# A decoder with 64 routed experts on one core: the final weighted sum divided among PE, VectorE and GpSimd, and the experts' transfers sent by SyncE in the order of the tiles

## The chip, the cores and the metric

The kernel runs on one core of a Trainium2 chip. The metric is the time on the device, in microseconds, of the whole program: two decoder layers, the second of which ends in a mixture of experts. The engines are named as in the profile: PE is the tensor engine, DVE is VectorE, ACT is ScalarE, POOL is GpSimd, SP is SyncE, which here only sends transfers. ACT and POOL can send transfers too; a "q" behind a name (SPq, ACTq) marks an engine's own queue of instructions. The kernel before took 856.12 us in the median of three runs.

## The reference, cut to what matters

Six blocks follow each other, each with a residual and a normalisation: attention, cross attention, a feed-forward block (layer 0), attention, cross attention, and the experts (layer 1). The change touches the last one alone. There are 1024 tokens (8 sequences of 128), 256 columns, 64 experts, and each token goes to its 8 best.

```python
logits = jnp.einsum('th,eh->te', x, gate_w)
probs = jax.nn.softmax(logits, axis=-1)
topk_w, topk_idx = jax.lax.top_k(probs, 8)
combine = (jax.nn.one_hot(topk_idx, 64) * topk_w[..., None]).sum(axis=1)
for each expert e:
    g = x @ w13_e[:128].T
    u = x @ w13_e[128:].T
    o = (silu(g) * u) @ w2_e.T
    acc = acc + combine[:, e][:, None] * o
x = layernorm(x + acc)
```

## The kernel before

Every token's row is scattered by POOL to `x5_slots` in device memory, into the 1024 places that each expert has there. The experts then work on tiles of 128 places. There are 127 tiles: one for each of the 64 experts (its first 128 places) and 63 extra ones, whose expert and first place a plan computes on PE and DVE while the first tiles run. An extra tile that the plan has no use for is given an address beyond the end; its transfers are conditional and are then skipped. PE does each tile's work all the same.

`ORDER` is the order of the tiles. The weights of 32 experts (`KEPT`) lie in SBUF from earlier stages. The other tiles, 32 own tiles of experts and 63 extra ones, get their weights (384 KB) through eight slots (`SLOTS`, tiles `w_slot`); `LOADS` lists them in order. Tiles 5 to 19 alternate between kept experts and the first eight loaded ones. Tiles 20 to 67 mix kept experts with 28 extra tiles. From tile 68 on, 24 own tiles with loaded weights are mixed with 35 extra ones, so every tile there loads weights. The input rows (136 KB) lie in six buffers (`WORK`).

PE's step j (`pe_experts`, L1702 on) transposes tile j (`turn`), multiplies tile j-1 by its first weights (`up`) and tile j-3 by its second (`down`). ACT copies the transposed rows and computes silu, DVE takes the product, picks the tokens' places (`pick`) and copies the result, and POOL scatters 128 rows to `y_slots`, one row for each of the 8 choices of each token.

Who sends what before the change:
- SP (`sp_experts`, L1680 on) sends the first eight weight blocks and the rows of tiles 0 to 5. Then it waits for the plan's table (`lines_set`) and goes over the extra tiles: it reads an address (`value_load`, L1695), sends that tile's weights once the eighth load before it has left its slot, and the rows of an extra tile j after the weight block whose slot belonged to tile j-8 (`AHEAD`).
- ACT (`act_experts`, L1744 on) sends the rows of the 58 own tiles from tile 6 on, five tiles ahead of its own place, and the weights of the 24 own tiles, five tiles after their slot's last user.

`load_rows` (L1664 on) waits until the buffer's last rows were transposed and picked; `load_weights` (L1657 on) until the slot's last `down` is done.

At the end, `sp_combine` waits for all scatters and sends eight transfers of 1 MB, one for each sequence: for every token its 8 rows from `y_slots`. The weighted sum is made on PE (`pe_combine`): ACT makes for each row index j a diagonal matrix of 128 weights, and PE adds the eight products of diagonal and rows in PSUM. DVE (`dve_combine`) adds the residual, takes statistics and their aggregate and adds epsilon (`begin`, lines L1899, L180, L182, L184). POOL takes the root (L188). DVE scales (`end`, L192), after the `begin` of the next sequence, and ACT sends the result out. Four lanes (`SUMS`) of buffers and PSUM banks are used in turn.

## Time and profile before

| | |
|---|---|
| median of 3 runs | 856.12 us (854.72 to 858.25) |
| the profiled execution | 856.72 us |
| its span on the core | 855.3 us |
| busy: PE, DVE, ACT, POOL | 769.4 us (90%), 531.2 us (62%), 345.7 us (40%), 290.8 us (34%) |
| mean granted PE clock | 0.948 of full speed |
| DMA | 112.21 MB, mean 131 GB/s |
| loop over the experts' tiles | from 605.95 us (first transposes) to some 812 us |
| final sum | from 816.31 us (first transfer sent) to 853.50 us (last DVE instruction) |

Times in the rows are microseconds from the start of the span, unless a mean or median is given in ns. Busy PE time is modelled for the ends of matmuls, since they are pipelined; the starts are read better than the ends.

### The profile page before, as it was taken

Reading aid. Unit: us, or ns where it says so; the run is one execution under the profiler, and the core shown is the slowest. Engines: PE = TensorE matmul, PEld = TensorE weight load, DVE = VectorE, ACT = ScalarE, POOL = GpSimd, SP = SyncE. Lnnn points to the kernel's source line nnn. Section 1 sums busy time; section 2 is a strip of 40 time slices with the busy share of each in tenths; the row PEclk is TensorE's granted clock in tenths of the full one; section 3 lists DMA queues with packets and bytes.
Section 4 is the critical chain, followed back from the end, with each engine's and each line's share of the span. In section 5 each row is a group of like instructions: output and inputs, shape, how many; then the busy total and the mean of one; then the engine's idle time right before and its main releaser. Section 6 shows DMA issues by size and latency. Waiting matters only on the chain.

```text
span 855.3 us, 16679 instructions
## 1 busy us (share of the span) xinstructions
PE 769.4 (90%) x5644; PEld 637.0 (74%) x5651; DVE 531.2 (62%) x1676; ACT 345.7 (40%) x899; POOL 290.8 (34%) x377
## 2 busy tenths in 40 slices
PE   5999998998899999999994899982699999899957
PEld 3667776776798998989893556541699998799856
DVE  2787677675566666666666588853366666555514
ACT  3354454443243544444442334331244443344433
POOL 1112212112124121212110007776366665566611
PEclk8899999999999999999997699987799999999979
DMA  9442520000121212411003046842478989855373
GB/s 256 105 145 74 178 62 13 7 1 1 38 87 44 85 45 71 137 53 60 25 13 112 5 157 202 319 147 94 126 232 287 298 287 294 298 153 173 117 320 128
DMA packets 62677, 112.21 MB, mean 131 GB/s; under 512 B 11244, under 2 KB 40410, under 8 KB 61313
## 3 DMA queue, kind: packets, MB, share of 16 engines
q1 hardware_dynamic: 40464, 75.23, 27.4%
q10 hardware_dynamic: 12960, 18.57, 7.2%
q0 software_dynamic: 9168, 17.35, 5.6%
q8 instruction: 46, 0.75, 0.4%
q14 instruction: 39, 0.31, 0.1%
HBM read 96.60 MB, written 35.52 MB: 154 GB/s over the span
## 4 chain that ended last, share of the span: by engine, by line
PE 80%; DVE 5%; DMA 5%; ACT 3%; issue 3%; POOL 2%; SPq 1%; DVEq 0%; POOLq 0%; ACTq 0%
PE ps L171 73%; PE ps L174 8%; DMA rows_e<-x_slots 2%; DMA dnb_sb<-in_dnb 1%; POOL x_slots L1470 1%; ACT pTc L1329 1%; DVE topc L1379 1%; DMA rowso<-y_slots 1%; POOL y_slots L1827 0%; SPq L1661 0%; DVE oT L1026 0%; ACT o_hi L963 0%; DMA x_slots<-rows_all,index_all 0%; DMA y_slots<-o_e,index_e 0%; DVE qc L1384 0%
## 5 line engine op out<-in xcount | busy, mean ns | idle before, releaser
L1827 POOL DMA_INDIRECT y_slots<-o_e,index_e x127 | 124.5, 980 | 88.3 <-issue 57.7
L171 PE MATMUL ps<-xT_e,w_slot 128*128 128x128 f32 x760 | 100.5, 275 | 0.1
L171 PEld LDWEIGHTS ps<-xT_e,w_slot 128*128 128x128 f32 x760 | 92.4, 192 | 0.4 <-issue 0.3
L1806 DVE TENSOR_TENSOR h_e<-ps,gate_e 128x128 f32<-128x128 f32 x127 | 37.0, 292 | 80.4 <-ACT gate_e L1763 79.8
L1757 ACT COPY xT_e<-ps 128x256 f32<-128x256 f32 x127 | 47.3, 372 | 72.9 <-PE ps L174 69.6
L1470 POOL DMA_INDIRECT x_slots<-rows_all,index_all x64 | 62.7, 979 | 28.7 <-issue 17.5
L174 PE MATMUL ps<-ident,rows_e 128*128 128x128 f32 x254 | 49.7, 278 | 19.1 <-DMA rows_e<-x_slots 19.1
L171 PE MATMUL ps<-x_hi,w_hi 128*128 128x512 f32 x192 | 62.2, 406 | 1.6 <-DVE x_lo L970 1.5
L1763 ACT ACTIVATE gate_e<-ps 128x128 f32<-128x128 f32 x127 | 35.3, 278 | 63.5 <-PE ps L171 62.7
L174 PEld LDWEIGHTS ps<-ident,rows_e 128*128 128x128 f32 x254 | 35.4, 143 | 33.0 <-DMA rows_e<-x_slots 21.2
L171 PE MATMUL ps<-x_lo,w_hi 128*128 128x512 f32 x192 | 59.8, 393 | 0.0
L171 PE MATMUL ps<-x_hi,w_lo 128*128 128x512 f32 x192 | 59.6, 392 | 0.0
L1329 ACT ACTIVATE pTc<-ps 128x1024 f32<-128x1024 f32 x32 | 32.8, 1024 | 61.4 <-PE ps L171 61.3
L171 PE MATMUL ps<-w_slot,h_e 128*128 128x256 f32 x190 | 56.7, 381 | 0.3 <-DVE o_e L1814 0.3
L1035 POOL TENSOR_TENSOR w_lo<-wh,w_hi 128x256 fp32r<-128x256 f32 x48 | 34.0, 736 | 62.0 <-ACT w_hi L931 62.0
L1814 DVE COPY o_e<-ps 128x256 f32<-128x256 f32 x127 | 52.6, 415 | 0.5 <-PE ps L171 0.4
L1054 POOL TENSOR_TENSOR wo_lo<-wo,wo_hi 128x256 fp32r<-128x256 f32 x15 | 11.0, 732 | 111.5 <-ACT wo_hi L957 111.5
L171 PE MATMUL ps<-qc,kkc 32*128 32x256 f32 x256 | 40.2, 435 | 7.1 <-ACT pTc L1329 6.5
L1379 DVE TENSOR_REDUCE topc<-ps 128x4 f32<-128x1024 f32 x32 | 38.1, 1219 | 13.5 <-PE ps L171 13.4
L171 PEld LDWEIGHTS ps<-x_lo,w_hi 128*128 128x128 f32 x192 | 36.4, 190 | 8.0
L171 PEld LDWEIGHTS ps<-x_hi,w_lo 128*128 128x128 f32 x192 | 36.3, 189 | 7.8
L171 PEld LDWEIGHTS ps<-x_hi,w_hi 128*128 128x128 f32 x192 | 34.4, 192 | 7.4 <-issue 1.8
(275 smaller groups left out, 1801.2 us busy)
## 6 DMA issues: line engine op xcount, KB each, us to landing
w_slot<-in_we SPq DMA_DIRECT2D x71, 384.0 KB
rows_e<-x_slots SPq DMA_DIRECT2D x69, 136.0 KB
w_slot<-in_we ACTq DMA_DIRECT2D x24, 384.0 KB
x_slots<-blank SPq DMA_DIRECT2D x4, 2176.0 KB, 9.2
rowso<-y_slots SPq DMA_DIRECT2D x8, 1024.0 KB, 12.4
rows_e<-x_slots ACTq DMA_DIRECT2D x58, 136.0 KB
w_kept<-in_we SPq DMA_DIRECT2D x20, 384.0 KB
wh<-in_wqkv SPq DMA_DIRECT2D x16, 384.0 KB, 3.5
```

Source lines behind the costliest of these rows:

```text
L171: return self.pe.matmul(out, lhsT, rhs, start=start, stop=stop, skip_group_check=shared)
L174: return self.pe.transpose(out, in_, self.ident[:, :])
L1035: return m.pool.tensor_tensor(t.w_lo[h % 2][:, :, which, :], t.wh[h % 2][:, :, which, :], t.w_hi[h % 2][:, :, which, :], ALU.subtract)
L1054: pool.tensor_tensor(t.wo_lo[:, :], t.wo[:, :], t.wo_hi[:, :], ALU.subtract).then_inc(*t.wo_lo_set.one)
L1329: act.activation(t.pT[e][:, 2 * j:2 * j + 2, :, :].rearrange("p g u m -> p (g u m)"), t.sT_bank.rearrange("p b n -> p (b n)"), ACT.Exp).th ...
L1379: dve.tensor_reduce(top_columns(L, mo)[:, 2 * j:2 * j + 2, :], t.s_bank[:, 2 * j:2 * j + 2, :].rearrange("p g (e n) -> p g e n", e=2), AX. ...
L1470: pool.indirect_dma_start(m.x5_slots, bass.IndirectOffsetOnAxis(ap=r.index[:, b, j:j + 1], axis=0), r.rows[:, b, :], None).then_inc(*t.row ...
L1757: act.copy(T.xT[:, :, :].rearrange("p k t -> p (k t)"), T.t_bank[:, 0:D]).then_inc(*t.rowsT.one)
L1763: act.activation(T.gate[:, :], T.g_bank[:, 0:P], ACT.Silu).then_inc(*t.gate.one)
L1806: dve.tensor_tensor(T.h[:, :], T.g_bank[:, P:2 * P], T.gate[:, :], ALU.mult).then_inc(*t.h.one)
L1814: dve.tensor_copy(T.o[:, :], T.o_bank[:, 0:D]).then_inc(*t.o.one)
L1827: pool.indirect_dma_start(m.y_slots, bass.IndirectOffsetOnAxis(ap=T.index[:, :], axis=0), T.o[:, :], None, bounds_check=TOK * TOPK - 1, oo ...
```

## The change

Three things are changed.

1. The final sum. PE adds rows 0 to 4 of the eight (`BY_PE` is 5), with five diagonals of ACT in place of eight. POOL multiplies row 7 by its weight and adds the residual (`add_last`), into a new tile `part` in each lane. DVE adds rows 5 and 6, each multiplied by its weight, to `part`, and then adds PSUM and `part`. POOL prepares two sequences ahead: `add_last(0)` and `add_last(1)` stand before the first root, `add_last(b + 2)` after root b.
2. ACT sends nothing in the loop over the tiles any more, and doesn't wait there for the scatter of the tokens.
3. SP sends all rows and weights in one loop over the tiles: at place j the rows of tile j+5, then the weights whose slot belonged to tile j-4. The addresses of extra tiles are read where they are first needed (`line_of`); the wait for the plan's table stands before the first of them, which is the weight block of tile 20, at place 9.

```diff
-AHEAD = 8
-SUMS = 4
+SUMS, BY_PE = 4, 5
...
 def sp_experts(...):
-    sp.wait_ge(*tp.lines_set(1))
-    todo = [j for j in LOADS if ORDER[j] >= NE]
-    for j in range(PLANNED - 3, TILES):
-        while todo and LOADS[LOADS.index(todo[0]) - SLOTS] + AHEAD <= j:
-            k = todo.pop(0)
-            at = place[k] = sp.value_load(r.extra_row[0:1, ORDER[k] - NE:ORDER[k] - NE + 1])
-            load_weights(t, sp, k, a["we"][bass.ds(at // ROWS, 1), :, :].rearrange("a p n -> (a p) n"), cond=at < NE * ROWS)
-        if ORDER[j] >= NE:
-            at = place.pop(j)
-            load_rows(t, sp, j, m.x5_slots[bass.ds(at, P), :], cond=at < NE * ROWS)
+    def line_of(j):
+
+        if j not in place:
+            if not place:
+                sp.wait_ge(*tp.lines_set(1))
+            place[j] = sp.value_load(r.extra_row[0:1, ORDER[j] - NE:ORDER[j] - NE + 1])
+        return place[j]
+
+    todo = LOADS[SLOTS:]
+    for j in range(1, TILES + 1):
+        ahead = j - 1 + WORK
+        if ahead < TILES and ORDER[ahead] < NE:
+            load_rows(t, sp, ahead, own_rows(m, ahead))
+        elif ahead < TILES:
+            at = line_of(ahead)
+            load_rows(t, sp, ahead, m.x5_slots[bass.ds(at, P), :], cond=at < NE * ROWS)
+        while todo and LOADS[LOADS.index(todo[0]) - SLOTS] + 4 <= j:
+            k = todo.pop(0)
+            if ORDER[k] < NE:
+                load_weights(t, sp, k, own_weights(a, k))
+            else:
+                at = line_of(k)
+                load_weights(t, sp, k, a["we"][bass.ds(at // ROWS, 1), :, :].rearrange("a p n -> (a p) n"), cond=at < NE * ROWS)
...
 def act_experts(...):
-    for k in range(PARTS):
-        act.wait_ge(*tc.row_out[k](NSEQ * TOPK // PARTS))
-    todo = [j for j in LOADS[SLOTS:] if ORDER[j] < NE]
...
-        ahead = j - 1 + WORK
-        if WORK <= ahead < TILES and ORDER[ahead] < NE:
-            load_rows(t, act, ahead, own_rows(m, ahead))
-        while todo and LOADS[LOADS.index(todo[0]) - SLOTS] + 5 <= j:
-            k = todo.pop(0)
-            load_weights(t, act, k, own_weights(a, k))
...
 def pe_combine(...):
-        for j in range(TOPK):
-            last = m.mm(t.bank[b % SUMS], L.diag[:, j, :], t.rows[b][:, j, :], start=j == 0, stop=j == TOPK - 1)
+        for j in range(BY_PE):
+            last = m.mm(t.bank[b % SUMS], L.diag[:, j, :], t.rows[b][:, j, :], start=j == 0, stop=j == BY_PE - 1)
...
-def pool_combine(m, t):
+def pool_combine(m, t, te, r):
+    pool = m.pool
+
+    def add_last(b):
+        L = t.lanes[b % SUMS]
+        pool.wait_ge(*t.rows_in[b](1))
+        if b >= SUMS:
+            pool.wait_ge(*t.summed(b - SUMS + 1))
+        c = m.pool_chain(pool.tensor_scalar(L.part[:, :], t.rows[b][:, TOPK - 1, :], r.weight_all[:, b, TOPK - 1:TOPK], None, ALU.mult))
+        pool.wait_ge(*c)
+        pool.tensor_tensor(L.part[:, :], L.part[:, :], r.rows[:, b, 0:D], ALU.add).then_inc(*t.last_added.one)
+
+    pool.wait_ge(*te.weight(NSEQ * TOPK + 1))
+    add_last(0)
+    add_last(1)
     for b in range(NSEQ):
-        m.pool.wait_ge(*t.norm6(max(2 * b, 1)))
+        pool.wait_ge(*t.norm6(max(2 * b, 1)))
         pool_norm_root(m, t.lanes[b % SUMS].mv).then_inc(*t.root6.one)
+        if b + 2 < NSEQ:
+            add_last(b + 2)
...
 def dve_combine(...), begin(b):
+        dve.wait_ge(*t.rows_in[b](1))
+        dve.wait_ge(*t.last_added(b + 1))
+        for j in range(BY_PE, TOPK - 1):
+            c = chain(dve.scalar_tensor_tensor(out=L.part[:, :], in0=t.rows[b][:, j, :], scalar=r.weight_all[:, b, j:j + 1],
+                                               in1=L.part[:, :], op0=ALU.mult, op1=ALU.add))
+            dve.wait_ge(*c)
         dve.wait_ge(*t.sum_ps(b + 1))
-        dve.tensor_tensor(L.acc[:, :], t.bank[b % SUMS], r.rows[:, b, 0:D], ALU.add).then_inc(*t.summed.one)
+        dve.tensor_tensor(L.acc[:, :], t.bank[b % SUMS], L.part[:, :], ALU.add).then_inc(*t.summed.one)
```

How the order of SP's instructions changes at the start of the tiles. `w_kept` and the eight `w_slot` blocks are sent before the tiles start; `rows_e` are a tile's rows; TENSOR_LOAD reads an extra tile's address, ISA computes with it. Before:

```order
L1661 DMA w_slot<-in_we 128x768 x8
L1669 DMA rows_e<-x_slots 128x272 x6
L1695 TENSOR_LOAD extra_row
L1661 ISA
L1661 DMA w_slot<-in_we 128x768
L1695 TENSOR_LOAD extra_row
L1661 ISA
L1661 DMA w_slot<-in_we 128x768
```

And after the change:

```order
L1660 DMA w_slot<-in_we 128x768 x8
L1668 DMA rows_e<-x_slots 128x272 x15
L1695 TENSOR_LOAD extra_row
L1660 ISA
L1660 DMA w_slot<-in_we 128x768
L1668 DMA rows_e<-x_slots 128x272 x2
L1695 TENSOR_LOAD extra_row
L1660 ISA
L1660 DMA w_slot<-in_we 128x768
L1668 DMA rows_e<-x_slots 128x272 x2
```

The rows of tiles 6 to 14 moved from ACT to SP ahead of the first address; those of tiles 15 to 19 moved behind it, two after each of the next weight blocks.

In the dense part, with extra tiles and own tiles that load weights, SP's order after the change is:

```order
L1660 DMA w_slot<-in_we 128x768
L1668 DMA rows_e<-x_slots 128x272
L1660 ISA
L1660 DMA w_slot<-in_we 128x768
L1695 TENSOR_LOAD extra_row
L1668 ISA
L1668 DMA rows_e<-x_slots 128x272
L1660 DMA w_slot<-in_we 128x768
```

Rows and weights alternate, the ones without ISA being those of own tiles, which stood on ACT before.

DVE's order of one sequence of the final sum, before:

```order
L192 TENSOR_SCALAR yo<-acco,mvo 128x256
L1899 TENSOR_TENSOR acco<-ps,rows_all 128x256
L180 BN_STATS statso<-acco 128x6
L182 BN_AGGR mvo<-statso 128x2
L184 TENSOR_SCALAR mvo<-mvo 128x1
```

DVE after the change, and POOL after it (before, POOL had only the line of the root, `mvo<-mvo,power`):

```order
L191 TENSOR_SCALAR yo<-acco,mvo 128x256
L1923 SCALAR_TENSOR_TENSOR parto<-rowso,weight_all,parto 128x256 x2
L1927 TENSOR_TENSOR acco<-ps,parto 128x256
L179 BN_STATS statso<-acco 128x6
L181 BN_AGGR mvo<-statso 128x2
L183 TENSOR_SCALAR mvo<-mvo 128x1
```

```order
L187 TENSOR_TENSOR mvo<-mvo,power 128x1
L1900 TENSOR_SCALAR parto<-rowso,weight_all 128x256
L1902 TENSOR_TENSOR parto<-parto,rows_all 128x256
L187 TENSOR_TENSOR mvo<-mvo,power 128x1
```

Two multiply-adds stand ahead of DVE's addition, and between two roots POOL has a multiplication and an addition.

## Rows read from the trace of the kernel before

**Rows 1.** Page, the chain that ended last: shares of the span by engine.

```profile
PE 80%; DVE 5%; DMA 5%; ACT 3%; issue 3%; POOL 2%; SPq 1%; DVEq 0%; POOLq 0%; ACTq 0%
```

**Rows 2.** Timeline of PE, transposes of tiles 14, 15, 69, 85: start, us, what.

```profile
628.40 0.38 PE L174 MATMUL ps<-ident,rows_e 128*128 128x128 f32 x2
629.95 0.38 PE L174 MATMUL ps<-ident,rows_e 128*128 128x128 f32 x2
...
713.42 0.38 PE L174 MATMUL ps<-ident,rows_e 128*128 128x128 f32 x2
...
743.77 0.44 PE L174 MATMUL ps<-ident,rows_e 128*128 128x128 f32 x2 [0.98 <-DMA rows_e<-x_slots]
```

**Rows 3.** Chain of waits at tiles 0 and 70: start, us, what.

```profile
603.85 2.05 DMA rows_e<-x_slots
...
709.30 0.34 SPq L1661
...
709.97 6.17 DMA rows_e<-x_slots
```

**Rows 4.** Windows of 10 us, 700 to 740: engines' busy us, PE clock, DMA share, GB/s.

```profile
700.00:710.00 10.00, 10.00 (x81) 9.40 (x80) 6.77 (x46) 4.20 (x13) 6.36 (x7) 1.00 0.88 284
710.00:720.00 10.00, 8.95 (x70) 8.05 (x69) 5.97 (x40) 3.79 (x12) 5.58 (x6) 1.00 0.86 273
720.00:730.00 10.00, 9.01 (x68) 7.80 (x66) 6.40 (x45) 3.55 (x12) 6.17 (x7) 1.00 0.96 323
730.00:740.00 10.00, 8.79 (x70) 8.29 (x71) 5.36 (x38) 3.62 (x11) 4.90 (x5) 1.00 0.95 312
```

**Rows 5.** Chain of waits in the final sum: start, us, what.

```profile
816.31 4.82 DMA rowso<-y_slots
...
853.09 0.41 DVE yo L192
```

**Rows 6.** Timeline of the final sum: PE as a whole, one sequence on DVE and POOL.

```profile
821.27 29.71 PE L171 MATMUL ps<-rowso,diago 128*128 128x256 f32 x128 [9.62 <-DMA rowso<-y_slots]
...
830.30 0.42 DVE L1899 TENSOR_TENSOR acco<-ps,rows_all 128x256 f32<-128x256 f32 x1 [2.16 <-PE ps L171]
...
831.51 0.41 DVE L192 TENSOR_SCALAR yo<-acco,mvo 128x256 f32<-128x256 f32 x1
831.67 0.64 POOL L188 TENSOR_TENSOR mvo<-mvo,power 128x1 f32<-128x1 f32 x1 [2.88 <-DVE mvo L184]
...
833.76 0.42 DVE L1899 TENSOR_TENSOR acco<-ps,rows_all 128x256 f32<-128x256 f32 x1 [1.84 <-PE ps L171]
```

**Rows 7.** Windows of 2 us in the final sum, columns as in rows 4.

```profile
822.00:824.00 2.00, 2.00 (x7) 1.55 (x6) 0.00 (x0) 0.00 (x0) 0.00 (x0) 0.50 1.01 422
...
834.00:836.00 2.00, 2.00 (x11) 1.77 (x10) 1.27 (x5) 0.99 (x4) 0.64 (x1) 1.00 0.99 402
```

**Rows 8.** Durations in ns (min/median/max) of a DVE multiply-add and a POOL copy.

```profile
L649 DVE SCALAR_TENSOR_TENSOR h<-h,hm,beta_sb x8: 467/474/870, 52.5 to 202.7; 64x256 f32<-64x256 f32 x8
...
L1439 POOL COPY kkc<-markc 128x256 f32<-128x256 f32 x6 | 2.6, 483 | 0.1
```

**Rows 9.** Timeline in layer 0, where DVE and POOL read SBUF together.

```profile
143.81 2.56 DVE L192 TENSOR_SCALAR x<-res,mv 128x256 f32<-128x256 f32 x1
144.14 2.08 POOL L1035 TENSOR_TENSOR w_lo<-wh,w_hi 128x256 fp32r<-128x256 f32 x3
...
202.54 0.72 POOL L725 TENSOR_TENSOR cx<-x,bdn_sb 128x256 f32<-128x256 f32 x1
202.68 0.87 DVE L649 SCALAR_TENSOR_TENSOR h<-h,hm,beta_sb 64x256 f32<-64x256 f32 x1 [0.33 <-POOL hm L719]
```

**Rows 10.** SP's queue: address loads (ns, min/median/max), and sends of the timeline (start, us).

```profile
L1695 SPq TENSOR_LOAD <-extra_row x63: 263/272/762, 627.3 to 799.0; - x63
...
628.21 3.40 SPq L1661 DMA_DIRECT2D w_slot<-in_we  x4
...
726.69 1.80 SPq L1669 DMA_DIRECT2D rows_e<-x_slots  x1
```

More of the change, by code:

```diff
@@ L1741, in pe_experts, with act_experts @@
         next(plan)
-def act_experts(m, a, t, tc):
+def act_experts(m, t):
     act = m.act
     act.preload_act_table(ACT.Silu)
-    for k in range(PARTS):
-        act.wait_ge(*tc.row_out[k](NSEQ * TOPK // PARTS))
-    todo = [j for j in LOADS[SLOTS:] if ORDER[j] < NE]
     for j in range(TILES + 1):
@@ L1852, in signals @@
         self.summed, self.norm6 = ev.compute("dve", "summed", NSEQ), ev.compute("dve", "norm6", 2 * NSEQ)
-        self.root6 = ev.compute("pool", "root6", NSEQ)
+        self.root6, self.last_added = ev.compute("pool", "root6", NSEQ), ev.compute("pool", "last_added", NSEQ)
 class CombineLane:
@@ L1858, in __init__ @@
         s = lambda name, shape, dt=F32: sb(f"{name}o_{n}", shape, dt)
-        self.diag, self.acc, self.y = s("diag", [P, TOPK, P]), s("acc", [P, D]), s("y", [P, D])
+        self.diag, self.acc, self.y = s("diag", [P, BY_PE, P]), s("acc", [P, D]), s("y", [P, D])
+        self.part = s("part", [P, D])
         self.stats, self.mv = s("stats", [P, 6]), s("mv", [P, 4])
@@ L1881, in pe_combine, with dve_combine @@
         pe.wait_ge(*t.rows_in[b](1))
-        for j in range(TOPK):
-            last = m.mm(t.bank[b % SUMS], L.diag[:, j, :], t.rows[b][:, j, :], start=j == 0, stop=j == TOPK - 1)
+        for j in range(BY_PE):
+            last = m.mm(t.bank[b % SUMS], L.diag[:, j, :], t.rows[b][:, j, :], start=j == 0, stop=j == BY_PE - 1)
         last.then_inc(*t.sum_ps.one)
-def pool_combine(m, t):
+def pool_combine(m, t, te, r):
[11 more added lines that the diff above has]
+    add_last(1)
     for b in range(NSEQ):
-        m.pool.wait_ge(*t.norm6(max(2 * b, 1)))
+        pool.wait_ge(*t.norm6(max(2 * b, 1)))
         pool_norm_root(m, t.lanes[b % SUMS].mv).then_inc(*t.root6.one)
-def dve_combine(m, t, r):
+        if b + 2 < NSEQ:
+            add_last(b + 2)
+def dve_combine(m, t, te, r):
     dve, chain = m.dve, m.dve_chain
+    dve.wait_ge(*te.weight(NSEQ * TOPK + 1))
     def begin(b):
         L = t.lanes[b % SUMS]
+        dve.wait_ge(*t.rows_in[b](1))
[4 more added lines that the diff above has]
+            dve.wait_ge(*c)
         dve.wait_ge(*t.sum_ps(b + 1))
-        dve.tensor_tensor(L.acc[:, :], t.bank[b % SUMS], r.rows[:, b, 0:D], ALU.add).then_inc(*t.summed.one)
+        dve.tensor_tensor(L.acc[:, :], t.bank[b % SUMS], L.part[:, :], ALU.add).then_inc(*t.summed.one)
         dve.wait_ge(*t.summed(b + 1))
@@ L1924, in diagonals @@
             act.wait_ge(*t.sum_ps(b - SUMS + 1))
-        for j in range(TOPK):
+        for j in range(BY_PE):
             last = act.activation(L.diag[:, j, :], m.ident[:, :], ACT.Copy, scale=r.weight_all[:, b, j:j + 1])
@@ L1965, in program_pe, with program_act @@
     pe_combine(m, s.to, s.te)
-def program_act(m, a, s, out):
+def program_act(m, s, out):
     act_layer0(m, s.t0, s.t1)
@@ L1972, in program_act @@
     act_cross1(m, s.tc, s.r, s.t1)
-    act_experts(m, a, s.te, s.tc)
+    act_experts(m, s.te)
     act_combine(m, s.to, s.te, s.r, out)
@@ L1982, in program_dve @@
     dve_experts(m, s.te, s.tp, s.r, dve_plan(m, s.tp, s.tc, s.r))
-    dve_combine(m, s.to, s.r)
+    dve_combine(m, s.to, s.te, s.r)
 def program_pool(m, s):
@@ L1991, in program_pool @@
     pool_experts(m, s.te)
-    pool_combine(m, s.to)
+    pool_combine(m, s.to, s.te, s.r)
 class Stages:
@@ L2032, in decoder @@
         program_pe(m, s)
-        program_act(m, a, s, out)
+        program_act(m, s, out)
         program_dve(m, s)
```

## The prediction

> **What bounds the kernel now.** I read the chain of waits first: 80% of the span hangs on the tensor engine (PE) [rows 1]. So a change counts only where PE waits, or where PE's own work gets shorter. Two places touch the change.
>
> The first is the loop over expert tiles. PE starts a tile every 1.55 us (the transposes of tiles 14 and 15 start at 628.40 and 629.95) and does so nearly everywhere. Between tile 69 (713.42) and tile 85 (743.77) it does not: 16 tiles take 30.35 us where 16 x 1.55 is 24.8, so 5.6 us are lost [rows 2]. The chain names the cause: the rows of tile 70 leave SP at 709.97, right behind a weight block sent at 709.30, and need 6.17 us to land; undisturbed rows need 2.05 us [rows 3]. The DMA engines are 86 to 96% busy there [rows 4]. So it is partly late sending, partly a crowded DMA.
>
> The second is the final sum. Its eight transfers start at 816.31, the first lands 4.82 us later, then PE works for 29.71 us without a gap [rows 6], and the last instruction on VectorE (DVE) ends at 853.50 [rows 5]. One sequence takes 3.46 us (the additions start at 830.30 and 833.76), of which DVE works from 830.30 to 831.92 and GpSimd (POOL) 0.64 us [rows 6]. PE is the bound, DVE and POOL are over half idle. PE runs on the lower level (0.50 granted, 1.2 GHz) for the first sequence, seven records in 2 us, and at 1.00 later, eleven; before the first sequence it had idled 9.62 us for the transfers [rows 6]. The DMA is full at 400 to 430 GB/s while they run [rows 7].
>
> **The final sum, worked out.** Removed: three of eight row products on PE, 3/8 of 3.46 us, so PE needs 2.16 us a sequence; and three of eight diagonals on ScalarE, which were never late. The transfers of 1 MB each, at 422 GB/s, come 2.49 us apart and need no more than before.
>
> Added on DVE, ahead of its old 1.62 us: two multiply-adds over 128x256. None of just this form stands in the trace; the nearest has the same 256 columns and both tensors in SBUF, on 64 partitions, and takes 0.47 us when nothing disturbs it [rows 8]. With 0.03 us of semaphore between instructions, DVE's sequence becomes 1.62 + 2 x 0.50 = 2.62 us, if nothing disturbs it. Added on POOL: a multiplication (bounds: the copy of 128x256 at 0.48 us [rows 8], the addition at 0.72 us [rows 9]; I take 0.7) and an addition of 0.72 us. With the root that is 2.1 us, below DVE's time, and the two preparations that stand ahead of root 0 give POOL a lead of two sequences. So POOL's own queue should hold nobody.
>
> What will disturb DVE is that both engines now read SBUF. The trace has the price. The multiply-add at 202.68 began 0.14 us after a POOL addition and took 0.87 us, where its median is 0.47: it ended 0.29 us after POOL did. Worse, the DVE instruction at 143.81 took 2.56 us instead of 0.41: three POOL additions ran from 144.14 to 146.22 and it ended only 0.15 us after the last [rows 9]. The Trainium skill states the same in "SBUF — State Buffer" (Who interferes with whom): a VectorE instruction with two SBUF inputs and a GpSimd one that reads SBUF take turns, and the loser waits for a whole instruction. By that page every overlap costs; these two rows agree, and my term is taken from them.
>
> The layout of one sequence in steady state, from the end of the previous begin: DVE does the old normalisation end, 0.41 us; POOL does the root, to +0.75. The first multiply-add runs from 0.45 to 0.93. POOL's multiplication waits for it and holds the port until about 1.65. The second multiply-add ends 0.29 after that, 1.94. Then addition, statistics, aggregate and epsilon, 1.27 us: 3.2 us a sequence. The lower bound is 2.62 (no collision), the upper 4.0: the second multiply-add waits through both POOL operations, as at 143.81 (0.93 + 0.7 + 0.72 + 0.3 + 1.3). I take 3.2, as POOL waits for its own semaphore between its two operations, which lets DVE in; the three at 144.14 had no such wait.
>
> The start: POOL needs 821.13 + 1.5 = 822.6 for the first part, DVE has its two products at 823.7, PE has five rows (ten records at the lower level) at about 824.7, and begin 0 ends at 826.0. Begin 1 ends at 828.3. Six more at 3.2 us give 847.5, and the tail behind the last epsilon (0.64 root, 0.41 end, gaps; 1.2 us) gives 848.7 against 853.5: **-4.8 us** (bounds -8.2 with 2.62 us, 0 with 4.0 us). The output transfer behind it stays.
>
> **The transfers of the experts.** ScalarE loses 58 row and 24 weight sends. It waited for PE anyway, so that is worth nothing. SP gets them, in the order of the tiles.
>
> *A new wait.* SP's first extra weight block, for tile 20, needs the plan's table. SP used to wait for it while ScalarE went on with the rows of tiles 6 to 19; now it stands after the rows of tile 14, and the rows of tile 15 stand behind it. The weight block leaves at 628.21 [rows 10], so rows 15 leave at 628.65 at the earliest and land at 630.7 if undisturbed. PE wants them at 629.95: 0.8 us lost. With the 384 KB block ahead of them in the same queue (0.93 us at 422 GB/s) it is **+1.7 us**, upper bound 2.5. Tiles 16 to 19 leave in time to follow at 1.55 us.
>
> *Earlier rows.* Call step n the stretch of PE that begins with the transposes of tile n. In the old program the rows of an extra tile R stand behind a weight block whose slot is released at the end of step R-5; now they stand ahead of it and need only the transposes of tile R-6. For tile 70 those are at 713.42 - 5 x 1.55 = 705.7, so the rows leave at about 706.2 instead of 709.97, 3.8 us sooner, and PE was 1.2 us late there. Own weights go two steps (3.1 us) sooner. But they share a crowded DMA: in 700 to 740 the engines have 0.12 + 0.14 + 0.04 + 0.05 of four 10 us windows free, 3.5 us [rows 4]. That can be filled; the order by need gives a little more. Bounds 0 and -5.6; I take **-4.0 us**.
>
> *SP's own work.* An extra tile costs SP the address, registers and weights, (3.40 - 0.34)/3 = 1.02 us, and rows, 0.67 us by the two sends of rows 3; an own tile about 0.9 us with weights. In the dense part 35 of 59 tiles are extra: 0.59 x 1.7 + 0.41 x 0.9 = 1.4 us a tile, under PE's 1.55. Nothing is charged, but the cover is thin: the address load takes 0.27 to 0.76 us, and a send has taken 1.80 us [rows 10].
>
> Here a rule speaks against any gain: "DMA: Bandwidth & Descriptors" of the Trainium skill (Issuing engines are not separate DMA queues) says all sends end on the same 16 engines and the issuer only saves issue time. By it alone this part would be 0 and the time 853.0. I count the earlier moment of sending, not another queue, so the page stands as a rival below.
>
> **Sum.** -4.8 + 1.7 - 4.0 = -7.1 us. The profiled execution took 856.72 us around a span of 855.3, close to the median of 856.12; so the span goes to 848.2 and the median to **849.0 us**.
>
> **Rivals.** A difference under 0.5% (4.3 us) can hardly be told from none.
> (a) No collisions, 2.62 us a sequence: 849.0 - 3.4 = 845.6. For it: beside POOL's small root the normalisation end kept its 0.41 us [rows 6]. Against it: rows 9. Chance 0.20.
> (b) DVE starves behind both POOL operations, 4.0 us: the sum gains nothing, 853.8. The row at 143.81 speaks for it, the wait inside POOL's pair against it. 0.12.
> (c) The crowded DMA gives nothing back: 849.0 + 4.0 = 853.0. For it, 96% busy in 720 to 730; against it, the 3.5 us free. 0.12.
> (d) Slower: SP becomes the pacemaker. It decides when SP's mean over tiles 20 to 86 passes 1.55 us, by address loads at 0.76 or sends held as at 1.80. At 1.75 us a tile, 67 x 0.2 = 13 us, less some 3 us of lead, is +10 us: 856.1 - 4.8 + 1.7 + 10 = 863. 0.06.
> (e) The multiply-add with two fp32 tensors in SBUF takes up to twice its time on 128 partitions: 0 to 0.47 us more for each; at 0.27 us more it is 3.75 us a sequence, and 852.4. Against it: the 0.47 us with two fp32 tensors in SBUF [rows 8] is hardly more than the 0.42 us of the plain addition over as many columns [rows 6]. The rule behind it is the Trainium skill's, "Vector Engine (DVE) Microarchitecture Reference" (Points that are easy to get wrong): two sources in SBUF that are not bf16 halve this instruction's throughput; by that rule the trace disagrees, on 64 partitions. 0.02.
> The forecast itself: 0.48, own range 846.5 to 851.5.
>
> **How the numbers follow.** Faster by over 0.5% is below 851.8: the forecast and (a), and a share of (b) and (c) where the other term is at its good end: 0.70. Within: the rest of (b), (c), (e) and an edge of the forecast, 0.24. Slower: (d), 0.06. The range 844.5 to 854.0 holds (b), (c) and most of (a).
>
> **What would show it.** Second multiply-adds of 0.9 to 1.0 us and first ones of 0.48; additions 3.2 us apart; PE with gaps in the sum; one idle of 1 to 2 us at tile 15; less than 2 us lost between tiles 69 and 85; the last normalisation 1.2 us after the last epsilon. It is wrong if additions are under 2.8 or over 3.6 us apart, or if SP's sends come later than before relative to PE.

## The result, and the profile after

The kernel after takes 845.88 us in the median of five runs (842.83 to 849.42), the kernel before, run beside it, 854.72 us (852.55 to 858.25). The ratio is 0.9885, with a 95% interval of 0.9851 to 0.9919: faster by 1.1%. The prediction was 849.0 us, 7.1 us less than before, or a ratio of 0.992. Its wide range, 844.5 to 854.0 us, holds the result; the forecast's own range, 846.5 to 851.5 us, ends 0.6 us above it. Timed once more (`after_again`, at the end of the experiments), the kernel after gave 845.69 us and 0.9896 [0.9855, 0.9938]. The profiled execution took 845.79 us around a span of 844.4 us, 10.9 us shorter than the span before.

The chain of waits, shares of the span by engine and by line (page of the kernel after), which answers to [rows 1]:

```profile
PE 80%; DVE 7%; ACT 3%; DMA 3%; issue 3%; POOL 2%; SPq 1%; DVEq 0%; POOLq 0%; ACTq 0%
PE ps L170 72%; PE ps L173 8%; DMA dnb_sb<-in_dnb 1%; POOL x_slots L1469 1%; ACT pTc L1328 1%; DVE topc L1378 1%; DVE parto L1923 1%; DMA rows_e<-x_slots 1%; DMA rowso<-y_slots 1%; POOL y_slots L1830 0%; DVE statso L179 0%; DVE acco L1927 0%; DVE oT L1025 0%; ACT o_hi L962 0%; DMA x_slots<-rows_all,index_all 0%
```

PE still carries 80%. New in the list are DVE's multiply-adds (`parto L1923`): in the final sum the chain has moved to DVE.

**Tile 15.** Timeline of PE: transposes of tile 14, its neighbours, and tile 15 (start, us, what; in brackets the idle time before and what ended it), answering to the first two lines of [rows 2]; below it SP's queue, and the wait that SP had before its first address load (us in total, times, longest).

```profile
627.28 0.38 PE L173 MATMUL ps<-ident,rows_e 128*128 128x128 f32 x2
627.50 1.06 PE L170 MATMUL ps<-xT_e,w_slot 128*128 128x128 f32 x8
628.39 0.60 PE L170 MATMUL ps<-w_slot,h_e 128*128 128x256 f32 x2
630.95 0.44 PE L173 MATMUL ps<-ident,rows_e 128*128 128x128 f32 x2 [1.96 <-DMA rows_e<-x_slots]
```

```profile
627.04 0.37 SPq L1660 DMA_DIRECT2D w_slot<-in_we  x1
627.50 0.85 SPq L1668 DMA_DIRECT2D rows_e<-x_slots  x2
```

```profile
SPq L1695 <- DVE extra_row L1573: 6.7, 1, 6.7
```

SP stands still for 6.7 us until DVE has written the table. The rows of tile 15 leave at 627.50, 0.46 us behind the weight block of tile 20, and PE begins at 630.95. The step takes 3.67 us instead of 1.55: 2.1 us lost.

**Tiles 69 to 85.** Their transposes, answering to the last two lines of [rows 2]:

```profile
714.48 0.38 PE L173 MATMUL ps<-ident,rows_e 128*128 128x128 f32 x2
...
739.22 0.38 PE L173 MATMUL ps<-ident,rows_e 128*128 128x128 f32 x2
```

The 16 tiles take 24.74 us instead of 30.35. No stall is left. The rows of tile 70 left 6.3 us before PE began tile 69, where they had left 3.5 us before it, and landed 3.1 us before PE took them. The windows of that stretch, answering to [rows 4] (busy us of PE, PEld, DVE, ACT, POOL; PE clock, DMA share, GB/s):

```profile
700.00:710.00 10.00, 10.00 (x79) 9.30 (x78) 6.40 (x45) 4.17 (x13) 6.26 (x8) 1.00 0.95 310
710.00:720.00 10.00, 10.00 (x81) 9.40 (x79) 7.01 (x48) 4.27 (x13) 6.59 (x7) 1.00 0.95 307
720.00:730.00 10.00, 10.00 (x79) 9.31 (x78) 6.42 (x46) 4.17 (x13) 6.03 (x8) 1.00 1.00 354
730.00:740.00 10.00, 10.00 (x81) 9.40 (x80) 6.90 (x46) 4.26 (x13) 6.59 (x7) 1.00 1.05 392
```

PE is busy for all 10 us of each window, and the DMA moved 354 and 392 GB/s where it had moved 323 and 312.

**The final sum.** From the chain of waits, answering to [rows 5]:

```profile
811.69 5.35 DMA rowso<-y_slots
...
842.21 0.41 DVE yo L191
```

From the first send to the last instruction, 842.62, it takes 30.93 us, where it took 37.19. One sequence on DVE and on POOL, answering to the sequence in [rows 6]:

```profile
825.30 1.21 DVE L1923 SCALAR_TENSOR_TENSOR parto<-rowso,weight_all,parto 128x256 f32<-128x256 f32 x2
826.54 0.42 DVE L1927 TENSOR_TENSOR acco<-ps,parto 128x256 f32<-128x256 f32 x1
827.00 0.43 DVE L179 BATCH_NORM_STATS2 statso<-acco 128x6 f32<-128x256 f32 x1
827.46 0.18 DVE L181 BATCH_NORM_AGGREGATE mvo<-statso 128x2 f32<-128x6 f32 x1
827.68 0.15 DVE L183 TENSOR_SCALAR mvo<-mvo 128x1 f32<-128x1 f32 x1
827.75 0.40 DVE L191 TENSOR_SCALAR yo<-acco,mvo 128x256 f32<-128x256 f32 x1
...
829.35 0.42 DVE L1927 TENSOR_TENSOR acco<-ps,parto 128x256 f32<-128x256 f32 x1
```

```profile
825.75 0.94 POOL L1900 TENSOR_SCALAR parto<-rowso,weight_all 128x256 f32<-128x256 f32 x1
826.77 0.73 POOL L1902 TENSOR_TENSOR parto<-parto,rows_all 128x256 f32<-128x256 f32 x1
```

The additions (L1927) stand 2.81 us apart here, 2.25 to 2.95 us in all. Within these sequences DVE waits for nobody. The pair of multiply-adds takes 1.21 us instead of 1.00 when POOL's multiplication begins beside it. The line as a whole (ns, min/median/max):

```profile
L1923 DVE SCALAR_TENSOR_TENSOR parto<-rowso,weight_all,parto x16: 476/485/731, 819.1 to 839.6; 128x256 f32<-128x256 f32 x16
```

**The budget of the span.** Tile 15 +2.1, tiles 69 to 85 -5.6, final sum -6.3, together -9.8 us. The other 1.1 us lie ahead of the tiles, which began at 604.86 instead of 605.95 us. In ten profiles from chips of like speed that moment lies between 604.9 and 611.3 us, whichever of the two loops follows, so nothing shows that the change caused them. So stages are compared below from trace to trace, and whole times only by their intervals.

### The profile page after: what moved, and what is told of

Read it like the earlier page. It is cut to its first block, busy times and chain, and to the rows that moved or that the text cites. A ratio compares the mean times of both kernels' runs of the same rounds, so it can differ in the third digit from the quotient of the medians.

```text
span 844.4 us, 16610 instructions
## 1 busy us (share of the span) xinstructions
PE 758.2 (90%) x5596; PEld 628.8 (74%) x5603; DVE 539.3 (64%) x1692; ACT 338.4 (40%) x875; POOL 304.3 (36%) x393
## 3 DMA queue, kind: packets, MB, share of 16 engines
q10 hardware_dynamic: 1152, 1.05, 0.4%
## 4 chain that ended last, share of the span: by engine, by line
PE 80%; DVE 7%; ACT 3%; DMA 3%; issue 3%; POOL 2%; SPq 1%; DVEq 0%; POOLq 0%; ACTq 0%
PE ps L170 72%; PE ps L173 8%; DMA dnb_sb<-in_dnb 1%; POOL x_slots L1469 1%; ACT pTc L1328 1%; DVE topc L1378 1%; DVE parto L1923 1%; DMA rows_e<-x_slots 1%; DMA rowso<-y_slots 1%; POOL y_slots L1830 0%; DVE statso L179 0%; DVE acco L1927 0%; DVE oT L1025 0%; ACT o_hi L962 0%; DMA x_slots<-rows_all,index_all 0%
```

## The experiments

Each kernel is timed beside the kernel before; "lost" is what the steps between the transposes of one tile and the next take beyond the undisturbed pace (16 steps in 24.73 us, 1.55 us each). Each entry rests on one profile. Tiles 2, 5 and 13 start 0.25 to 0.5 us late in every profile, the kernel before's too, and are left out below. The ratios are those of the record, with their intervals; they are not always the quotient of the two medians.

### The two halves alone

The final sum alone, on the kernel before; `pool_combine`, `dve_combine` and the rest of the sum as after the change, `sp_experts` and `act_experts` as before:

```diff
-SUMS = 4
+SUMS, BY_PE = 4, 5
...
-        for j in range(TOPK):
-            last = m.mm(t.bank[b % SUMS], L.diag[:, j, :], t.rows[b][:, j, :], start=j == 0, stop=j == TOPK - 1)
+        for j in range(BY_PE):
+            last = m.mm(t.bank[b % SUMS], L.diag[:, j, :], t.rows[b][:, j, :], start=j == 0, stop=j == BY_PE - 1)
```

> The kernel before with the new final sum alone; the experts' transfers are sent as before. My theory: the two halves add up and do not touch each other. From the first transfer of the sum (sent) to the last VectorE instruction it takes 30.9 us as with the whole change, 37.2 before, so -6.3 us; tile 15 starts 1.55 us after tile 14, and the 16 tiles from 69 to 85 lose the 5.6 us again. Total -6.3 us, ratio about 0.993. Rival: the change in the sum is worth less by itself, because its transfers follow a differently loaded DMA; then the stretch is over 32 us.

Measured: 846.57 us, ratio 0.9898 [0.9853, 0.9944]. The sum takes 31.01 us, 6.2 less than before, with additions 2.54 to 2.83 us apart. Nothing is lost at tile 15, as nothing there was touched. The loss in tiles 69 to 85 was 3.7 us, although this code is that of the kernel before, which lost 5.6 in its own profile. Three of the stalls, tiles 70, 78 and 85:

```profile
715.97 0.44 PE L174 MATMUL ps<-ident,rows_e 128*128 128x128 f32 x2 [1.00 <-DMA rows_e<-x_slots]
...
729.79 0.44 PE L174 MATMUL ps<-ident,rows_e 128*128 128x128 f32 x2 [1.09 <-DMA rows_e<-x_slots]
...
741.68 0.44 PE L174 MATMUL ps<-ident,rows_e 128*128 128x128 f32 x2 [0.17 <-DMA rows_e<-x_slots]
```

So the old loop's loss differs from run to run, and the 5.6 us that the change took away are one draw, 3.7 another. The half alone was expected at a ratio of about 0.993, which its interval holds. By the whole time it can't be told from the full change (0.9898 against 0.9885); what the transfers add shows in the stages and in the next run.

The transfers alone, on the kernel before: the loop of `sp_experts` as after the change, the final sum as before, and in `act_experts`:

```diff
-        ahead = j - 1 + WORK
-        if WORK <= ahead < TILES and ORDER[ahead] < NE:
-            load_rows(t, act, ahead, own_rows(m, ahead))
-        while todo and LOADS[LOADS.index(todo[0]) - SLOTS] + 5 <= j:
-            k = todo.pop(0)
-            load_weights(t, act, k, own_weights(a, k))
```

> The kernel before with the new order of the experts' transfers alone; the final sum is the old one. My theory: tile 15 starts 3.67 us after tile 14 (2.1 us lost), tiles 69 to 85 lose nothing (5.6 us gained), net -3.5 us, ratio about 0.996; the final sum takes 37.2 us from first send to last VectorE instruction. Rival: the release of ScalarE from sending also shortens the sum or the steps; then a tile's step is under 1.545 us or the sum under 36.5 us.

Measured: 852.01 us, ratio 0.9942 [0.9901, 0.9983]. Tile 15 loses 2.1 us, tiles 69 to 85 take 24.73 us with nothing lost, the sum takes 37.22 us. Both effects of the transfers belong to this half, and neither half needs the other one. The sum of the two ratios' gains, 1.0 and 0.6%, is 1.6%; the whole change measured 1.15%, which lies inside the intervals.

### The wait for the table

```diff
-        while todo and LOADS[LOADS.index(todo[0]) - SLOTS] + 4 <= j:
+        while todo and j >= 14 and LOADS[LOADS.index(todo[0]) - SLOTS] + 4 <= j:
```

On the kernel after: SP reads the first address behind the rows of tile 19 instead of those of tile 14.

> The changed kernel, but SP sends no weight block of the loop before place 14, so that the wait for the plan's table stands behind the rows of tile 19 and not behind those of tile 14. My theory: the 2.1 us at tile 15 are the wait for the table alone. Tile 15 starts 1.55 us after tile 14, nothing is lost later (the first extra weights had over 10 us to spare), so 2.1 us less than the changed kernel: some 843.8 us where that has 845.9, ratio to before about 0.986. Rival: the four weight blocks that are then sent together push the rows of tiles 20 to 24 back, and part of the 2 us returns there.

Measured: 843.69 us in the median of four runs, ratio 0.9824 [0.9740, 0.9909]. PE's transposes of tiles 13, 14 and 15 follow each other after 1.60 and 1.55 us:

```profile
631.42 0.44 PE L173 MATMUL ps<-ident,rows_e 128*128 128x128 f32 x2
...
633.02 0.38 PE L173 MATMUL ps<-ident,rows_e 128*128 128x128 f32 x2
...
634.57 0.38 PE L173 MATMUL ps<-ident,rows_e 128*128 128x128 f32 x2
```

Apart from the three tiles named above, no tile from 0 to 126 starts late, and SP no longer waits for the table at all. So the 2.1 us come from the place of that wait, with its weight block, ahead of the rows of tiles 15 to 19. How they divide between the late sending and the block sent just ahead isn't separated by this run, which moves both. The transfers held back until then are not missed later, but the margin is thin: the rows of tile 21 landed 0.6 us before PE took them here, and 0.04 us before it in the repaired version below. The ratio rests on four runs, and the kernel after was not timed beside them.

### What cured the crowded stretch: one queue, or the moment of sending?

Two theories. Theory 1: rows and weights are sent earlier, and it matters little by whom. Theory 2: one queue, in the order of need, keeps a later tile's block from going ahead of an earlier tile's. First, half of the step with both queues kept, on the kernel before: the rows of extra tiles ahead of the weight block, ScalarE unchanged.

```diff
-AHEAD = 8
+AHEAD = 9
...
-    for j in range(PLANNED - 3, TILES):
+    for j in range(PLANNED - 3, TILES + 2):
...
-            at = place[k] = sp.value_load(r.extra_row[0:1, ORDER[k] - NE:ORDER[k] - NE + 1])
+            at = line_of(k)
```

> The kernel before with one edit: SP sends the rows of extra tiles ahead of the weight block and not behind it (AHEAD 9 in place of 8), one step of 1.55 us or more earlier. ScalarE still sends the rows and weights of own tiles, as late as before, and there are two queues. Theory 1 (the moment of sending counts, for rows): the loss between tiles 69 and 85 falls from 5.6 us to under 2. Theory 2 (the own weights that ScalarE sent two steps later count as well; they had 0.1 to 0.7 us to spare): the loss of rows goes, but waits for own weights at tiles 76, 79, 81, 83 take its place, and 2 to 4 us stay. Theory 3 (one queue in the order of need counts): the loss stays at 5 us or more. The final sum as before.

Measured: 855.01 us (the profiled execution 857.74), ratio 0.9946 [0.9898, 0.9993]. In tiles 69 to 85 1.9 us are lost. No tile waits for its rows; they land at least 0.7 us early. What is left are waits for own weights, which ScalarE still sends late:

```profile
737.04 1.13 PE L171 MATMUL ps<-xT_e,w_slot 128*128 128x128 f32 x8 [1.12 <-ACT xT_e L1762]
```

The bracket names the copy of the transposed rows, but that had ended at 736.33. The weights of tile 79, sent by ScalarE at 730.64, landed at 736.95, and PE began 0.09 us later. So the earlier rows are part of the cure and not all of it. The second half, besides the edit above, in `act_experts`: ScalarE's weights two steps earlier, still from two queues:

```diff
-        while todo and LOADS[LOADS.index(todo[0]) - SLOTS] + 5 <= j:
+        while todo and LOADS[LOADS.index(todo[0]) - SLOTS] + 3 <= j:
```

> The kernel before with two queues kept, the rows of extra tiles ahead of the weight block (as in rows_early) and, new here, ScalarE sending the weights of own tiles two steps earlier, as SyncE does after the change. Theory 1, the moment of sending counts, whoever sends: the 1.36 + 0.47 us lost at tiles 81 and 78 in rows_early, which hung on ScalarE's weights with a slack of 0.1 us, go, tiles 69 to 85 take 24.7 to 25.3 us and the time is 5 to 6 us under the kernel before's loop, thus about 850. Theory 2, one queue in the order of need counts: the loss stays at 2 to 4 us. No wait at tile 15 in either case, since SyncE's rows of tile 15 are not moved.

This run says nothing on it. It fell on a chip where the kernel before itself needs 932.02 us, and this one 930.23 (ratio 0.9980 [0.9941, 1.0020]). All four kernels profiled on that chip lost time all over the loop (here 5.6 us in tiles 69 to 85). In the trace of the kernel without GpSimd's part (below, same chip) the rows of these tiles had landed 3 to 6 us early, and ScalarE stands still:

```profile
697.19 0.28 ACT L1772 ACTIVATE gate_e<-ps 128x128 f32<-128x128 f32 x1 [1.05 <-PE ps L170]
699.43 0.37 ACT L1766 COPY xT_e<-ps 128x256 f32<-128x256 f32 x1 [1.97 <-PE ps L173]
699.70 0.28 ACT L1772 ACTIVATE gate_e<-ps 128x128 f32<-128x128 f32 x1
```

What the copy at 699.43 waits for, the transposes begun at 696.9, was long there. Why the engine paused is not recorded, and stays open. The kernel before was not profiled on this chip. The same kernel again, on a chip where the kernel before needs 854.12 us:

> The same kernel as both_early. In that run, on a chip where the kernel before needs 932 us, ScalarE stood still for about 2 us every few tiles in all kernels, and nothing could be read from tiles 69 to 85. If this run is free of that (the kernel before near 855 us), the same two expectations hold: by the moment of sending, tiles 69 to 85 take 24.7 to 25.3 us and the time is about 850; by the single queue, 2 to 4 us stay lost.

Measured: tiles 69 to 85 take 24.73 us, from 718.79 to 743.52, nothing lost:

```profile
718.79 0.38 PE L174 MATMUL ps<-ident,rows_e 128*128 128x128 f32 x2
...
743.52 0.38 PE L174 MATMUL ps<-ident,rows_e 128*128 128x128 f32 x2
```

```profile
720.00:730.00 10.00, 10.00 (x79) 9.30 (x78) 6.51 (x45) 4.18 (x13) 6.28 (x7) 1.00 1.00 336
730.00:740.00 10.00, 10.00 (x81) 9.40 (x81) 6.90 (x48) 4.27 (x13) 6.45 (x7) 1.00 1.02 377
```

In this stretch theory 1 holds, by one profile against five of the single queue (24.73 or 24.74 us in each): two queues do as well as one if they send as early. The least slack, 0.34 us for rows, is less than after the change (1.35 us), and 0.98 us were lost at tile 96, so one queue in order may still leave more room. In the whole time it hardly shows: 851.34 us, ratio 0.9974 [0.9943, 1.0005], an interval that doesn't exclude no change. Its profiled execution (858.16 us) was at the slow end of its runs and had started the tiles 5.3 us later than the profile of the kernel before. The ratio doesn't contradict the stage: by the two draws of the old loss, 3.7 or 5.6 us, less some 1.1 us lost behind tile 85, 2.6 to 4.5 us should be gained, an estimate that gives ratios of 0.997 to 0.995, all inside the interval. The losses of the old loop on this chip were not profiled, so it confirms nothing either.

The opposite test, on the kernel with the late table: one queue kept, but from tile 14's place on the weights go first and then the rows of a tile one step nearer.

```diff
-    for j in range(1, TILES + 1):
-        ahead = j - 1 + WORK
+    for j in range(1, TILES + 2):
+        ahead = j - 2 + WORK if j > 14 else j - 1 + WORK
-        if ahead < TILES and ORDER[ahead] < NE:
-            load_rows(t, sp, ahead, own_rows(m, ahead))
-        elif ahead < TILES:
-            at = line_of(ahead)
-            load_rows(t, sp, ahead, m.x5_slots[bass.ds(at, P), :], cond=at < NE * ROWS)
         while todo and j >= 14 and LOADS[LOADS.index(todo[0]) - SLOTS] + 4 <= j:
...
+        if j == 15:
+            pass
+        elif ahead < TILES and ORDER[ahead] < NE:
+            load_rows(t, sp, ahead, own_rows(m, ahead))
+        elif ahead < TILES:
+            at = line_of(ahead)
+            load_rows(t, sp, ahead, m.x5_slots[bass.ds(at, P), :], cond=at < NE * ROWS)
```

> The kernel after, first address read at tile 14 or later (as in table_late), one queue, but from there on at each place the weights go first and then the rows of a tile one step nearer, so that each row block leaves 1.55 us later and behind a weight block. If the moment counts, tiles 69 to 85 lose again 1 to 4 us, all of it in waits for rows, and the slack of rows falls by 2 to 3 us. If the single queue alone had cured the loss, they take 24.7 us as in the kernel after. Final sum as after, 31 us from first send to last instruction.

This one fell on the slow chip as well: 929.33 us against 932.02 (ratio 0.9954 [0.9919, 0.9989]), 4.3 us lost in tiles 69 to 85, where every profile of that chip loses 2.5 us or more. Nothing follows for the loop. Again, on the other chip:

> The same kernel as rows_late, for the same reason. If the moment counts, tiles 69 to 85 lose 1 to 4 us in waits for rows; if the single queue does, they take 24.7 us. Final sum 31 us from first send to last instruction.

Measured: 849.10 us, ratio 0.9952 [0.9921, 0.9984]. One queue, and losses are back: 1.2 us in tiles 69 to 85, where PE begins tiles 78 to 84 only 0.04 to 0.20 us after their rows land, and 1.7 us in tiles 15 to 69. The windows show where PE is short:

```profile
720.00:730.00 10.00, 10.00 (x81) 9.40 (x80) 6.92 (x48) 4.27 (x13) 6.47 (x7) 1.00 0.96 326
730.00:740.00 10.00, 9.51 (x71) 8.01 (x70) 5.98 (x43) 3.64 (x12) 5.93 (x7) 1.00 1.04 368
```

So a single queue does not cure it by itself. This run is the weaker of the two sides, though: the edit sends rows later and also puts them behind a weight block that is needed a step after them, so it breaks the order of need together with the moment. And with tile 70's rows leaving 3.6 us before tile 69 starts, as late as in the kernel before (3.5), that tile is not late here; only 1.2 us are lost, not 3.7 or 5.6, since the weights still leave early. What carries the conclusion is the run with two queues and early sending: no common queue is needed. Early rows with late own weights left 1.9 us lost, early weights with late rows 1.2 us.

### The price of sharing in the final sum

On the kernel after, GpSimd's multiplication and addition are taken out. The product of row 7 is left out of the result with them, so this kernel computes less:

```diff
-    pool.wait_ge(*te.weight(NSEQ * TOPK + 1))
-    add_last(0)
-    add_last(1)
...
-        if b + 2 < NSEQ:
-            add_last(b + 2)
...
-        dve.wait_ge(*t.last_added(b + 1))
...
-                                               in1=L.part[:, :], op0=ALU.mult, op1=ALU.add))
+                                               in1=L.part[:, :] if j > BY_PE else r.rows[:, b, 0:D], op0=ALU.mult, op1=ALU.add))
```

> The kernel after, but GpSimd's multiplication and addition are left out of the final sum, and the product of row 7 with them (it is left out of the output's sum; VectorE's first multiply-add adds the residual). What is measured is the price of the two engines' sharing. If the collisions cost the 0.25 us that the trace of the kernel after shows in half of the sequences, VectorE's additions stand 2.55 to 2.6 us apart throughout and first send to last instruction falls by 0.7 to 1.3 us from 30.9. If GpSimd's work costs more than it shows there (late parts, not the port), it falls by 2 us or more. If transfers or the tensor engine bound the sum, it falls by less than 0.4 us.

It ran on the slow chip (923.94 us against 932.02, ratio 0.9996 [0.9952, 1.0040]), whose pauses are in the loop; the sum shows none. It takes 29.68 us, and the additions stand 2.56 to 2.58 us apart after the first. No multiply-add takes over 0.49 us:

```profile
L1917 DVE SCALAR_TENSOR_TENSOR parto<-rowso,weight_all,rows_all x8: 476/480/484, 885.4 to 906.7; 128x256 f32<-128x256 f32 x8
L1917 DVE SCALAR_TENSOR_TENSOR parto<-rowso,weight_all,parto x8: 485/485/485, 885.9 to 907.2; 128x256 f32<-128x256 f32 x8
```

The second and the last addition, of this kernel and then of the kernel after:

```profile
892.30 0.42 DVE L1921 TENSOR_TENSOR acco<-ps,parto 128x256 f32<-128x256 f32 x1
907.72 0.42 DVE L1921 TENSOR_TENSOR acco<-ps,parto 128x256 f32<-128x256 f32 x1
```

```profile
823.59 0.42 DVE L1927 TENSOR_TENSOR acco<-ps,parto 128x256 f32<-128x256 f32 x1
840.13 0.42 DVE L1927 TENSOR_TENSOR acco<-ps,parto 128x256 f32<-128x256 f32 x1
```

The last six intervals add up to 15.42 us here and to 16.54 in the kernel after. The sharing costs 1.1 us in six sequences, 0.19 us each. The chip is not the reason: `rows_late`, with GpSimd's part and on the same slow chip, needs 16.40 us for them.

The same place without GpSimd and complete: six rows for PE, two for DVE, besides the edits above.

```diff
-SUMS, BY_PE = 4, 5
+SUMS, BY_PE = 4, 6
...
-        for j in range(BY_PE, TOPK - 1):
+        for j in range(BY_PE, TOPK):
```

> The kernel after with the rows divided six to the tensor engine, two to VectorE and none to GpSimd. The tensor engine then needs 6/8 of 3.46 = 2.6 us a sequence, VectorE 2.56 undisturbed. If the two bounds merely coincide, additions stand 2.6 to 2.7 us apart, no multiply-add takes over 0.5 us, and the sum takes 30.3 to 31 us, the same or up to 0.7 us less than after. If the start decides (first part while the tensor engine is still at its lower level), one more row costs 0.5 us once and the sum takes 31.4 us.

Measured: 926.35 us on the slow chip, ratio 0.9918 [0.9878, 0.9957]. The additions stand 2.58 to 2.60 us apart, the last six intervals 15.54 us, and the sum takes 30.39 us. PE's 2.59 us (six eighths of 3.45) and DVE's 2.56 nearly coincide.

### The repaired version, and the kernel after once more

The late table and the six and two rows together.

> The kernel after with the first address read at tile 14 or later (table_late) and the rows of the sum divided six to the tensor engine and two to VectorE, none to GpSimd (pe6). Expected against the kernel after: 2.1 us less at tile 15, 0.5 us less in the sum (30.4 for 30.9 us from first send to last instruction), thus some 2.6 us less, 843, a ratio of 0.985 to the kernel before. If the tensor engine's longer part of the sum costs as much as the collisions did, only the 2.1 us stay.

Measured: 843.43 us (838.49 to 851.01, 12 runs), ratio 0.9901 [0.9862, 0.9940]. The loop is clean: 1.54 us at tile 15, 24.73 us in tiles 69 to 85, no late tile but the three that always are. The sum takes 31.50 us, not 30.4. Its steady part is as foreseen (2.59 us apart six times); the start is slow. Windows of 2 us from PE's first matmul on, of this kernel and then of the kernel after (the clock is the last figure but two):

```profile
815.00:817.00 2.00, 2.00 (x5) 1.64 (x6) 0.89 (x2) 0.00 (x0) 0.00 (x0) 0.50 1.02 426
817.00:819.00 2.00, 2.00 (x6) 1.55 (x6) 0.00 (x0) 0.00 (x0) 0.00 (x0) 0.50 1.00 422
819.00:821.00 2.00, 2.00 (x7) 1.61 (x6) 0.45 (x2) 0.00 (x0) 0.00 (x0) 0.53 1.03 434
```

```profile
817.20:819.20 2.00, 2.00 (x5) 1.64 (x6) 0.11 (x1) 0.00 (x0) 1.66 (x2) 0.50 1.03 434
819.20:821.20 2.00, 2.00 (x8) 1.66 (x7) 0.86 (x2) 0.00 (x0) 1.49 (x2) 0.67 1.00 422
```

PE waited 9.7 and 10.1 us for the first rows and begins at 0.50 (1.2 GHz) in both. Here it reached the upper level 6.0 us after its start, there 3.4 us, with 13 matmuls instead of 8 at the low level. In the kernel after this rise came early, which hid part of what the sum costs there. The six profiles of the five-two-one division show the spread: with the rise 3.1 to 4.0 us after PE's start the sum takes 30.2 to 30.9 us (`rows_late_2`, the two of the kernel after), with the rise after 5.3 to 6.0 us 31.0 to 31.5 us (`sum_only`, `rows_late`, `table_late`). `table_late`, whose rise came as late as here, takes 31.51 us, the same as the repaired version. So the 1.0 us that the steady part gains is not seen in the sum as a whole: with six rows PE has more to do while it is still at the low level.

> The kernel after once more, unchanged, on another chip or at another time, for the spread of its stages. If the readings of the first profile hold: 2.1 us lost at tile 15, nothing lost in tiles 69 to 85 (24.7 us), additions of the sum 2.55 to 2.95 us apart, and from first send to last instruction between 30.2 and 31.5 us, by how soon the tensor engine's clock rises. Against best (ratio 0.990 to the kernel before) it should be some 2 to 3 us slower, thus 0.992 to 0.994; if it comes out at 0.9885 again, the repaired version is not measurably better.

Measured: 845.69 us, ratio 0.9896 [0.9855, 0.9938]. Tile 15 loses 2.1 us, tiles 69 to 85 take 24.74 us, additions stand 2.26 to 2.95 us apart (2.55 to 2.95 was expected), and the sum takes 30.67 us. The stages of the loop repeat to 0.1 us, the sum to 0.3; the ratio is not the 0.992 to 0.994 that I had expected. By the traces the repaired version saves 2.1 us at tile 15; the 1.0 us in the steady sum goes at its start. By the times it is not shown to be faster: 0.9901 against 0.9885 and 0.9896, with intervals 0.8% wide, and never on one chip together.

## Why the prediction was right

The number came out within the range, and the three terms have the right signs and places. One step of the sum's mechanism failed, by the prediction's own sign ("wrong if additions are under 2.8 or over 3.6 us apart"), and part of the closeness is luck, as said below.

- **The bound in the sum.** Foreseen: DVE takes PE's place, PE gets gaps. Confirmed; the chain runs along DVE from the second sequence on, and PE has three gaps of some 0.4 us. The term was -4.8 us and measured -6.3. Mis-sized was the collision: the second multiply-add was put at 0.9 to 1.0 us and 3.2 us a sequence. It takes 0.69 to 0.73 us in four sequences of eight and 0.48 in the others; the mean interval is 2.69 us. The step that failed is "POOL's multiplication holds the port until about 1.65; the second multiply-add ends 0.29 after that". At 825.75 the multiplication begins and runs to 826.69, yet the multiply-add beside it is over at 826.51. It lost 0.2 us and, as far as GpSimd's recorded end can be trusted, did not wait for it. The two rows at 143.81 and 202.68 [rows 9] were read as a queue behind whole instructions; for this pair the runs don't bear that out. The same goes for the Trainium skill's "SBUF — State Buffer" (Who interferes with whom), by whose rule the loser waits for a whole instruction: here that would be up to 0.94 us, and 0.2 to 0.25 us was lost. What decides the smaller price stays open.
- **Two errors in the sum's term that partly cancel.** Six steady sequences at 3.2 us were 19.2 us and measured 16.5, 2.7 us less. Against that the start was 1.2 us slower than counted: the first transfer took 5.35 us and not 4.82, and the first addition came 4.3 us after it landed and not 3.6. The net is the 1.5 us by which the term was short.
- **GpSimd.** Its multiplication takes 0.92 to 1.21 us, not 0.7 and outside my bounds (0.48 to 0.72), and its addition 0.72 as read. It was hidden as argued: DVE waited for it only ahead of the first sequence, where PE's five products came later still (first addition at 821.3). The 0.93 us of the very first one, at 817.22, had no DVE instruction beside it, so the time is its own and not a collision's.
- **Tile 15.** Foreseen +1.7, at most 2.5; measured +2.1. The rows left 0.46 us behind the weight block, as said (0.44), and took 3.4 us to land, where 2.05 undisturbed plus 0.93 had been counted. Undoing the order took it away.
- **Tiles 69 to 85.** Foreseen -4.0 with a bound of -5.6; measured -5.6, the whole loss of the profile before. The term was too small because I had counted only the 3.5 us of free share as what the DMA could still give and a little for the order; fed in time it moved 354 and 392 GB/s at a share of 1.00 and 1.05. Tile 70's rows left 2.9 us sooner relative to tile 69, not 3.8. The reason given, earlier sending and not another queue, was tested and holds, the second queue being as good when it sends as early. Since the old loss was 3.7 us in another profile, -4.0 is as good a mean as -5.6.
- **SP as pacemaker (rival d).** It did not come: with SP sending everything, no tile after 15 started late in the five profiles of this loop on chips of like speed (`after`, `after_again`, `loads_only`, `table_late`, `best`).
- **The other rivals.** (a), no collisions, gave 845.6 and is nearest in time, but not in mechanism: half the sequences do collide, at about half the price. (b), (c) and (e) are refuted by 2.25 to 2.95 us a sequence, by the empty list of waits in the crowded stretch, and by 0.485 us for the multiply-add on 128 partitions. For (e) the trace of the kernel before had a nearer row than the one used: L654 has the same size, with one of its two tensors in PSUM (`res<-ps,b_sb,cx`), and takes as long.

```profile
L654 DVE SCALAR_TENSOR_TENSOR res<-ps,b_sb,cx x8: 475/482/484, 56.1 to 205.7; 128x256 f32<-128x256 f32 x8
```

So for this form the rule in the Trainium skill's "Vector Engine (DVE) Microarchitecture Reference" (Points that are easy to get wrong), that two sources in SBUF which are not bf16 halve the throughput, is not borne out: 0.485 us with both in SBUF stand against 0.482 with one.

Of the 3.8 us by which the span fell further than foreseen, the sum gives 1.5, the crowded stretch 1.6, tile 15 takes 0.4 back, and 1.1 is the earlier start of the tiles, which the change doesn't explain.

## What to carry to other kernels

A queue that mixes transfers needed at once with those that wait for a late result should place the wait behind the urgent ones; the position of one wait, and of the block behind it, cost 2.1 us here. In a stretch where the DMA is full, ask first how early each transfer leaves, and only then from which queue. When work is divided among engines, a partner on the same memory may cost little, but see whether leaving it out costs anything at all: six rows and two did as well as five, two and one.

## What the runs showed of the hardware that was not expected

- When DVE and GpSimd read SBUF together, either can be the one that loses: in the sequence at 833.68 both multiply-adds kept 0.48 us and GpSimd's multiplication took 1.21 us instead of 0.94.
- In the kernel after GpSimd's multiplication of 128x256 by a column takes 0.94 us in the median, its addition of two such tensors 0.72.
- With rows and weights always waiting, the 16 DMA engines moved 392 GB/s in a 10 us window at a share of 1.05; with gaps in the sending, 312 GB/s at 0.95 [rows 4].
- After 9.5 to 10.1 us without work, PE began the sum at the lower level and stayed there for 3.1 us (`rows_late_2`) to 6.0 us (`table_late`, the repaired version), differing between executions. By estimate the 2.6 us more at half the rate, from the kernel after to the repaired one, cost PE 1.3 us of its work.
- One chip ran every one of these programs some 9% slower, with pauses of ScalarE of about 2 us that no record explains.
